# Layer 1's attention: who issues the small transfers of its softmax sums

## The chip, the cores and the metric
The program runs on one core of one Trainium2 chip. The metric is the device time of a run in microseconds (us); of several runs the median is given. One run was recorded by the hardware profiler, and its trace is read below.

The engines of the core each work through their own queue of instructions in order: TensorE (PE in the rows; its weight loads are PEld), VectorE (DVE), ScalarE (ACT), GpSimd (POOL) and SyncE (SP; SPq is its queue). They meet at semaphores alone.

## The reference
A decoder of four layers over x, 2 batches x 1024 positions x 256 channels. Each layer adds self-attention, cross-attention and a feed-forward part, with a layer norm behind each. The change lies in the self-attention of layer 1 alone: 16 query heads, 4 key/value heads, head size 64, rotary positions, causal.

```python
q, k, v = x @ Wq, x @ Wk, x @ Wv          # 16, 4 and 4 heads of 64, rotated q and k
att = softmax(mask(q @ k.T / 8))          # causal, per head
x = layernorm(x + (att @ v) @ Wo)
```

## The kernel before
`packed_attention` works in 32 **steps**. A step is 2 heads, one batch and 512 queries. Steps alternate: a step over the first 512 positions has 4 **units** (a unit is 128 keys against the step's queries), one over the last 512 has 8. They are called short and long steps here. In units that the causal mask cuts, fewer queries are left: 512, 384, 256, 128 over the last four units of every step, so for both heads together 1024, 768, 512 and 256 columns.

For each unit PE computes transposed scores (L914, mask L917); ACT takes the exponential twice, once to float16 (`ph_hi`, L1031) and once to float32 (`probs`, L1032; the trace calls this buffer `res`); the difference of the two is `ph_lo`. GpSimd subtracts it for three units of four (L834), VectorE for the fourth (L1093). PE then multiplies by the values (`values`, L935) and adds up the probabilities with a matrix of ones (`totals`, L955), two units behind and two units at a time.

Beside this, two steps ahead, PE computes the scores again in rows (L886, mask L889) only for VectorE to take their maxima (L1055). PE and VectorE take turns through two PSUM banks: item `a` of PE waits until VectorE is done with item `a - 2`. The maxima are turned (L894), split in two halves (L1063, L1065) and sent by SP into the query operand (L806). The order of these items among the units is laid out ahead by `Plan.lay`.

The end of a step goes through several engines:

- ACT waits for the step's `totals` and copies the output (`o_raw`, L1007) and the row sums (`sums`, L1011) out of PSUM. In its queue this stands ahead of the exponentials of unit 2 of the next step (`LAG = 2`).
- The sums lie along the free dimension of two partitions for each half. Two DMAs spread them over 128 partitions x 8 (`y_col`); they are GpSimd's (L839; L845 for the last step), in its queue behind unit 2's subtraction.
- VectorE adds the halves (L1076) and inverts (L1078) at the end of the next step's last unit.
- A DMA brings the inverse back into two rows (`r_row`, GpSimd's L842, behind the subtraction of unit 1 of the step after; L848 for the last two).
- PE spreads the rows over the partitions (L898, three steps behind), and VectorE multiplies the output by it (L1069).

SP's queue holds, for each step, the two transfers of the maxima, and at every second step nine loads of queries and keys for a coming pair of steps (L791, L794).

Of the kernel before, what the change touches and what calls it, by code (L numbers as in the profile page):

```python
# [683 lines left out]
def packed_attention(k, name, plan, G, stack, q, kk, v_all, o_t, kv_of=1, q_pos=None, k_pos=None, gate=None, split=False, scratch=None):  # L684
# [22 lines left out]
    S, U = len(steps), len(units)  # L707
    PR = G // 2
    GB = T // QC
    LEAD, INV, SPR = plan.lead, plan.invert_at, plan.spread_at  # L710
    pairs = not own_sums and G == 2
    SR = P // 4
    SLOTS = 5 if split else 4 if pairs else 3
    LAG = 2 if split else 0
    FULL = 3

    def by_dve(n):

        return n % 4 == 3
# [6 lines left out]
    KEEP = SPR + 1  # L726
# [15 lines left out]
    with Phase(k, name) as ph:  # L742
# [9 lines left out]
        sums = None if own_sums else scratch[:, in_scratch:in_scratch + 2 * QC].rearrange("p (i q) -> p i q", q=QC) if split else ph.sb("sums", [P, 2, QC])  # L752
        ones = None if own_sums else ph.sb("ones", [P, SR], F16 if split else F32)
        y_col, r_col = ph.sb("y_col", [P, 2, KEEP, YC]), ph.sb("r_col", [P, KEEP, YC])
        r_row = ph.sb("r_row", [P, KEEP, QC])
# [4 lines left out]
        y_ld = [ph.sem(f"y_ld{i}") for i in range(KEEP)]  # L760
        r_ld = [ph.sem(f"r_ld{i}") for i in range(KEEP)]
# [5 lines left out]
        s_ = ph.s  # L767
        EV = 1 if own_sums else 2
        n_clear = 1 if own_sums else 2

        with nc.Block() as block:

            @block.sync
            def _(sp):

                def load(tb):

                    st = steps[2 * tb]
                    slot = tb % LOADS
                    if tb >= LOADS:  # L780
                        sp.wait_ge(s_["b_done"], PR * plan.first_unit[2 * (tb - LOADS) + 2])
                    else:
                        sp.wait_ge(s_["k_filled"], slot + 1)
                        sp.wait_ge(s_["q_filled"], slot + 1)
                    h0, b = st.heads[0], st.batch
                    sp.sem_inc(s_["loading"], 1)
                    hk = h0 // kv_of
                    for c, r0, part in stack.q_parts:
                        rows = q[part][h0 * dh:(h0 + G) * dh].rearrange("(h d) n -> d h n", d=dh)
                        for g in range(GB):  # L790
                            sp.dma_start(qs[r0:r0 + dh, slot, c, g, :, :], rows[:, :, b * T + g * QC:b * T + (g + 1) * QC]).then_inc(ld[slot], 16)  # L791
                    for c, r0, part in stack.k_parts:
                        rows = kk[part][hk * dh:(hk + KH) * dh].rearrange("(h d) n -> d h n", d=dh)
                        sp.dma_start(ks[r0:r0 + dh, slot, :, c, :], rows[:, :, b * plan.n_keys:(b + 1) * plan.n_keys]).then_inc(ld[slot], 16)  # L794
                    if q_pos is not None:
                        for g in range(GB):
                            rows = q_pos[h0:h0 + G, :, b * T + g * QC:b * T + (g + 1) * QC]
                            sp.dma_start(qs[99:102, slot, 0, g, :, :], rows.rearrange("h r n -> r h n")).then_inc(ld[slot], 16)
                        sp.dma_start(ks[96:99, slot, :, 0, :], k_pos[h0:h0 + G, :, b * T:(b + 1) * T].rearrange("h r n -> r h n")).then_inc(ld[slot], 16)

                def maximum_rows(s):

                    st = steps[s]
                    sp.wait_ge(s_["maxed"], turned_at[s])
                    for i, m in enumerate((mh, ml)):
                        sp.dma_start(qs[R + i:R + i + 1, (s // 2) % LOADS, stack.m_chunk, st.q0 // QC, :, :], m[:, s % LEAD, :]).then_inc(m_ld[s % LEAD], 16)  # L806

                sp.dma_start(spread[:], k.a["c_spread"][0 if G == 4 else 1]).then_inc(s_["c_ld"], 16)
                for tb in range(min(LOADS, TBS)):
                    load(tb)  # L810
                for s in range(S):
                    maximum_rows(s)
                    tb = (s - LEAD - 1) // 2 + LOADS
                    if s >= LEAD and s % 2 and tb < TBS:
                        load(tb)

            @block.gpsimd
            def _(pool):
                for i in range(LOADS):
                    pool.memset(ks[stack.m0:R + 2, i, :, stack.m_chunk, :], 1.0).then_inc(s_["k_filled"], 1)  # L820
                pool.wait_ge(s_["k_filled"], LOADS)
                pool.memset(r_row[:], 0.0).then_inc(s_["cleared"], 1)
                if not own_sums:
                    pool.wait_ge(s_["cleared"], 1)
                    pool.memset(ones[:], 1.0).then_inc(s_["cleared"], 1)
                pool.wait_ge(s_["cleared"], n_clear)
                if split:
                    pool.wait_ge(s_["v_upper"], 1)
                    pool.tensor_tensor(v_lo[:], v_all[:], v_hi[:], ALU.subtract).then_inc(s_["v_lower"], 1)
                    for n, (s, u) in enumerate(units):  # L830
                        w = QC - u.off
                        if not by_dve(n):
                            pool.wait_ge(s_["exps"], n + 1)
                            pool.tensor_tensor(ph_lo[:, n % SLOTS, :, 0:w], probs[:, n % FULL, :, 0:w], ph_hi[:, n % SLOTS, :, 0:w], ALU.subtract).then_inc(s_["low_pool"], 1)  # L834
                        at = n - plan.first_unit[s]
                        if at == LAG and s:
                            pool.wait_ge(s_["evac"], EV * s)
                            for half in range(2):
                                pool.dma_start(y_col[:, half, (s - 1) % KEEP, :], sums[half * G * SR:(half + 1) * G * SR:SR, (s - 1) % 2, :]).then_inc(y_ld[(s - 1) % KEEP], 16)  # L839
                        if at == 1 and s >= 2:  # L840
                            pool.wait_ge(s_["recips"], s - 1)
                            pool.dma_start(r_row[0:G, (s - 2) % KEEP, :], r_col[:, (s - 2) % KEEP, :]).then_inc(r_ld[(s - 2) % KEEP], 16)  # L842
                    pool.wait_ge(s_["evac"], EV * S)
                    for half in range(2):
                        pool.dma_start(y_col[:, half, (S - 1) % KEEP, :], sums[half * G * SR:(half + 1) * G * SR:SR, (S - 1) % 2, :]).then_inc(y_ld[(S - 1) % KEEP], 16)  # L845
                    for s in (S - 2, S - 1):
                        pool.wait_ge(s_["recips"], s + 1)
                        pool.dma_start(r_row[0:G, s % KEEP, :], r_col[:, s % KEEP, :]).then_inc(r_ld[s % KEEP], 16)  # L848
                    return

                for n in range(S + INV - 1):
                    if n < S:
                        s, st = n, steps[n]
                        pool.wait_ge(s_["evac"], EV * (s + 1))
                        if own_sums:
                            pool.dma_start(y_col[:, 0, s % KEEP, :], o_raw[dh:P:MR, s % RAW, :]).then_inc(y_ld[s % KEEP], 16)
                        for half in range(0 if own_sums else parts_of(s)):
                            pool.dma_start(y_col[:, half, s % KEEP, :], sums[half * G * SR:(half + 1) * G * SR:SR, s % 2, :]).then_inc(y_ld[s % KEEP], 16)
                        if gate is not None:
                            b0 = st.batch * T + st.q0  # L860
                            raw = o_raw[:, s % RAW, :]
                            pool.tensor_tensor(raw, raw, gate[:, st.turn, b0:b0 + QC], ALU.mult).then_inc(s_["gated"], 1)
                    s = n - INV + 1
                    if s >= 0:
                        pool.wait_ge(s_["recips"], s + 1)
                        pool.dma_start(r_row[0:G, s % KEEP, :], r_col[:, s % KEEP, :]).then_inc(r_ld[s % KEEP], 16)
# [133 lines left out]
            def _(act):  # L1000

                def evacuate(s):

                    act.wait_ge(s_["values"], plan.first_unit[s + 1])
                    if s >= RAW:
                        act.wait_ge(s_["maxed"], spread_of[s - RAW])
                    act.activation(o_raw[:, s % RAW, :], X[s % 2], ACT.Copy).then_inc(s_["evac"], 1)  # L1007
                    if not own_sums:
                        if s >= 2:
                            act.wait_ge(y_ld[(s - 2) % KEEP], y_full[s - 2])  # L1010
                        act.activation(sums[:, s % 2, :], Y, ACT.Copy).then_inc(s_["evac"], 1)  # L1011

                if KR < P:
                    act.wait_ge(s_["zeroed"], 1)
# [2777 lines left out]
```

## Time and profile before

| | us |
|---|---|
| median of 3 runs | 3721.22 |
| lowest, highest | 3717.83, 3728.87 |
| profiled run, its own time | 3708.89 |
| its span in the trace | 3707.1 |
| layer 1's attention in the span | about 1283 to 1858 |

Over the whole span PE is busy for 2768.1 us (75%), VectorE 1767.4 (48%), ACT 1260.5 (34%), GpSimd 790.3 (21%). No ACT queue is among the DMA queues: all transfers of the kernel are issued by SP or GpSimd. Times in the rows are us from the span's start; "idle before" is how long an engine did nothing before that instruction, with the name of what it had waited for.

### The profile page before, as it was taken

To read this page: it belongs to the slowest core of one execution; us is meant where nothing else is said; L and a number is where in the kernel's file an instruction comes from. 1 tells how busy PE (TensorE), PEld (TensorE's weight loads), DVE (VectorE), ACT (ScalarE), POOL (GpSimd) and SP (SyncE) were. 2 spreads that over 40 slices of the span, in tenths; PEclk is the share of its full clock that TensorE was granted. 3 is DMA by queue.
4 is the path that set the end of the run, shared out by engine and by line. 5 is a ranking of instruction groups with operands and counts; after the bars stand their busy time and mean duration, and the time that the engine had idled before them with its cause. 6 is when DMAs were issued, how large, how long until landed. Compare 5 with 4: busy or idle time off the path is not lost. (4 is left out here: it accounts for less than half of the span.)

```text
span 3707.1 us, 42704 instructions
## 1 busy us (share of the span) xinstructions
PE 2768.1 (75%) x15498; PEld 1576.0 (43%) x15498; DVE 1767.4 (48%) x3896; ACT 1260.5 (34%) x2532; POOL 790.3 (21%) x648
## 2 busy tenths in 40 slices
PE   6789995786715688788774878787566888668696
PEld 3333333565512333333362455464342333346575
DVE  4566645244654555555424458144323767523412
ACT  4234441332411255565502300223212445335421
POOL 0101110134372456665600100002001000001100
PEclk9889997897867889999986979898787899789898
DMA  2211101600553322222102100200004020110132
GB/s 98 82 38 37 37 2 41 223 20 12 165 99 83 97 39 40 29 41 41 3 18 66 24 15 11 100 10 20 12 4 90 13 36 14 38 60 1 38 107 69
DMA packets 157229, 183.04 MB, mean 49 GB/s; under 512 B 34654, under 2 KB 123311, under 8 KB 156259
## 3 DMA queue, kind: packets, MB, share of 16 engines
q1 hardware_dynamic: 144547, 166.82, 15.6%
q0 software_dynamic: 12480, 13.57, 3.9%
q8 instruction: 122, 2.00, 0.2%
q14 instruction: 80, 0.66, 0.1%
HBM read 121.81 MB, written 61.59 MB: 49 GB/s over the span
## 5 line engine op out<-in xcount | busy, mean ns | idle before, releaser
L834 POOL TENSOR_TENSOR l1a_p_lo<-res,l1a_p_hi 128x1024 f16<-128x1024 f32 x144 | 266.9, 1855 | 211.5 <-ACT res L1032 211.3
L1055 DVE TENSOR_REDUCE l1a_nmax<-ps 128x1 f32<-128x512 f32 (+3 forms) x384 | 200.1, 551 | 149.0 <-PE ps L889 119.3
L1055 DVE TENSOR_REDUCE l0a_nmax<-ps 128x1 f32<-128x512 f32 (+3 forms) x384 | 200.9, 555 | 122.2 <-PE ps L889 93.3
L1055 DVE TENSOR_REDUCE l3a_nmax<-ps 128x1 f32<-128x512 f32 (+3 forms) x384 | 199.3, 553 | 80.5 <-PE ps L889 65.8
L1039 ACT ACTIVATE l0a_probs<-ps 128x1024 f32<-128x1024 f32 (+1 forms) x192 | 145.7, 812 | 229.7 <-PE ps L917 182.1
L1031 ACT ACTIVATE l1a_p_hi<-ps 128x1024 f16<-128x1024 f32 x192 | 158.1, 823 | 161.0 <-PE ps L917 135.3
L1039 ACT ACTIVATE l3a_probs<-ps 128x1024 f32<-128x1024 f32 (+1 forms) x192 | 148.8, 810 | 184.1 <-PE ps L917 147.9
L886 PE MATMUL ps<-l1a_ks,l1a_qs 128*128 128x512 f16 (+3 forms) x384 | 124.5, 345 | 95.7 <-DVE l1a_nmax L1055 74.7
L914 PE MATMUL ps<-l1a_qs,l1a_ks 128*128 128x512 f16 (+3 forms) x768 | 167.6, 333 | 21.9 <-ACT res L1032 21.9
L889 PE MATMUL ps<-mask,ident_b 128*128 128x128 bf16 x768 | 171.7, 231 | 0.0
L886 PE MATMUL ps<-l3a_ks,l3a_qs 126*128 126x512 f16 (+3 forms) x384 | 126.7, 354 | 44.9 <-DVE l3a_nmax L1055 20.0
L1032 ACT ACTIVATE res<-ps 128x1024 f32<-128x1024 f32 x192 | 158.7, 826 | 0.0
L917 PE MATMUL ps<-mask_t,ident_b 128*128 128x128 bf16 x768 | 154.5, 222 | 0.0
L886 PE MATMUL ps<-l0a_ks,l0a_qs 102*128 102x512 f16 (+3 forms) x384 | 124.9, 353 | 29.2 <-DMA l0a_ks<-l_k_pos 16.9
L2485 PE MATMUL ps<-x_m_all,res 128*128 128x512 f32 (+2 forms) x256 | 97.6, 528 | 21.2 <-PEq L111 14.2
L1667 PE MATMUL ps<-res,l1p_w 128*128 128x512 f32 x160 | 83.1, 681 | 34.9 <-DVE l1p_tmp L1730 22.9
L886 PEld LDWEIGHTS ps<-l1a_ks,l1a_qs 128*128 128x128 f16 x384 | 37.6, 98 | 168.2 <-DVE l1a_nmax L1055 111.5
L886 PEld LDWEIGHTS ps<-l0a_ks,l0a_qs 102*128 102x128 f16 x384 | 36.0, 99 | 169.7 <-DVE l0a_nmax L1055 122.9
L886 PEld LDWEIGHTS ps<-l3a_ks,l3a_qs 126*128 126x128 f16 x384 | 36.5, 99 | 156.4 <-DVE l3a_nmax L1055 113.0
L914 PEld LDWEIGHTS ps<-l1a_qs,l1a_ks 128*128 128x128 f16 x768 | 61.9, 99 | 92.9 <-issue 35.6
L914 PE MATMUL ps<-l3a_qs,l3a_ks 128*128 128x512 f16 (+3 forms) x384 | 99.4, 330 | 0.9 <-ACT l3a_probs L1039 0.9
L914 PE MATMUL ps<-l0a_qs,l0a_ks 104*128 104x512 f16 (+3 forms) x384 | 99.0, 331 | 0.5 <-ACT l0a_probs L1039 0.5
(671 smaller groups left out, 6279.2 us busy)
## 6 DMA issues: line engine op xcount, KB each, us to landing
f_w<-in_L_ffn_w_dram SPq DMA_DIRECT2D x16, 1024.0 KB, 7.4
f_slots<-x0a_zeros SPq DMA_DIRECT2D x32, 256.0 KB, 4.9
f_xe<-f_slots SPq DMA_DIRECT2D x32, 256.0 KB, 3.0
f_ys<-f_y SPq DMA_DIRECT2D x32, 256.0 KB, 2.3
l1a_qs<-l_q_h SPq DMA_DIRECT2D x64, 128.0 KB
d_wall<-in_L_ffn_W_dram SPq DMA_DIRECT2D x3, 2112.0 KB
l0a_qs<-l_q_h SPq DMA_DIRECT2D x32, 128.0 KB
l0a_ks<-l_k_h SPq DMA_DIRECT2D x16, 256.0 KB
```

What stands on the lines that cost most here:

```text
L834: pool.tensor_tensor(ph_lo[:, n % SLOTS, :, 0:w], probs[:, n % FULL, :, 0:w], ph_hi[:, n % SLOTS, :, 0:w], ALU.subtract).then_inc(s_["low_ ...
L886: ins = pe.matmul(sa[:, col:col + f.w], qs[0:stack.max_rows, slot, 0, st.q0 // QC, f.p, q0:q0 + P], ks[0:stack.max_rows, slot, f.p if KH > ...
L889: ins = pe.matmul(sa[:, f.w - P:f.w], k.ident_b[:], k.mask[:], start=False, stop=True)
L914: ins = pe.matmul(SB[x % 2][:, half, 0:w], ks[0:r, slot, p if KH > 1 else 0, d, u.key:u.key + KR], qs[0:r, slot, d, st.q0 // QC, p, u.off: ...
L917: ins = pe.matmul(SB[x % 2][:, half, 0:P], k.ident_b[:], k.mask_t[:], start=False, stop=True)
L1031: act.activation(ph_hi[:, n % SLOTS, :, 0:w], SB[n % 2][:, :, 0:w], ACT.Exp)
L1032: act.activation(probs[:, n % FULL, :, 0:w], SB[n % 2][:, :, 0:w], ACT.Exp).then_inc(s_["exps"], 1)
L1039: act.activation(probs[0:KR, n % SLOTS, 2 * pr:2 * pr + 2, 0:w], SB[x % 2][:, :, 0:w], ACT.Exp).then_inc(s_["exps"], 1)
L1055: dve.tensor_reduce(nmax[:, s % LEAD, f.chunk, f.p, f.tile:f.tile + f.n], src, AX.X, ALU.max, negate=True).then_inc(s_["maxed"], 1)
L1667: ins = pe.matmul(slot[j % 2][:, c0:c0 + w], lhsT, rhs, start=n == 0, stop=n == len(terms) - 1)
L2485: ins = pe.matmul(S[:, c:c + w], xs[:, d, t * P:(t + 1) * P], m_all[:, d, i, c:c + w], start=d == 0, stop=d == DC - 1)
```

## The change
In layer 1's attention (`split`), ACT issues the two DMAs of the sums itself, right behind its own copy of them and after waiting for that copy's semaphore; unit 2's exponentials come behind them. SP issues the DMA of the inverse, after the transfers of the maxima of its iteration `s` and ahead of that iteration's loads, for step `s - 3`; the last three follow at the end. GpSimd's queue keeps its subtractions alone. The other attentions keep their code.

```diff
@@ SP @@
+                def inverse_row(s):
+                    sp.wait_ge(s_["recips"], s + 1)
+                    sp.dma_start(r_row[0:G, s % KEEP, :], r_col[:, s % KEEP, :]).then_inc(r_ld[s % KEEP], 16)
                 for s in range(S):
                     maximum_rows(s)
+                    if split and s >= LEAD + INV:
+                        inverse_row(s - LEAD - INV)
                     tb = (s - LEAD - 1) // 2 + LOADS
                     if s >= LEAD and s % 2 and tb < TBS:
                         load(tb)
+                for s in range(S - LEAD - INV, S) if split else ():
+                    inverse_row(s)
@@ GpSimd @@
-                        at = n - plan.first_unit[s]
-                        if at == LAG and s:
-                            pool.wait_ge(s_["evac"], EV * s)
-                            for half in range(2):
-                                pool.dma_start(y_col[...], sums[...]).then_inc(y_ld[(s - 1) % KEEP], 16)
-                        if at == 1 and s >= 2:
-                            pool.wait_ge(s_["recips"], s - 1)
-                            pool.dma_start(r_row[...], r_col[...]).then_inc(r_ld[(s - 2) % KEEP], 16)
...
@@ ACT, evacuate(s) @@
                         act.activation(sums[:, s % 2, :], Y, ACT.Copy).then_inc(s_["evac"], 1)
+                        if split:
+                            act.wait_ge(s_["evac"], EV * (s + 1))
+                            for half in range(2):
+                                act.dma_start(y_col[:, half, s % KEEP, :], sums[half * G * SR:(half + 1) * G * SR:SR, s % 2, :]).then_inc(y_ld[s % KEEP], 16)
```

## Rows read from the trace of the kernel before

**Rows 1.** Busy time of each engine over 28 full steps, and TensorE's granted clock.
```profile
core 0: us, PE busy (x) PEld busy (x) DVE busy (x) ACT busy (x) POOL busy (x), PEclk, DMA share, GB/s
1340.00:1823.00 483.00, 390.37 (x3235) 180.99 (x3234) 263.45 (x531) 278.50 (x394) 299.49 (x211) 0.98 0.23 34
```

**Rows 2.** Waits of the stage: engine and line, releaser: us, times, longest.
```profile
POOL l1a_p_lo L834 <- ACT res L1032: 211.3, 122, 18.1
...
PE ps L886 <- DVE l1a_nmax L1055: 72.9, 59, 2.5
DVE l1a_y_col L1076 <- DMA l1a_y_col<-res: 51.3, 15, 4.2
...
PE ps L914 <- ACT res L1032: 21.9, 32, 1.8
```

**Rows 3.** Timeline, copies in a short step: start, us, engine, line.
```profile
1514.36 0.59 ACT L1011 ACTIVATE res<-ps 128x512 f32<-128x512 f32 x1
...
1514.74 0.60 SPq L794 DMA_DIRECT2D l1a_ks<-l_k_h  x1
...
1514.83 0.61 ACT L1031 ACTIVATE l1a_p_hi<-ps 128x512 f16<-128x512 f32 x1
...
1515.31 0.62 ACT L1032 ACTIVATE res<-ps 128x512 f32<-128x512 f32 x1
...
1516.07 1.02 PE L914 MATMUL ps<-l1a_qs,l1a_ks 128*128 128x512 f16 x4 [0.45 <-ACT res L1032]
```

**Rows 4.** Timeline, the end of the same short step.
```profile
1517.12 1.58 POOL L839 DMA_DIRECT2D l1a_y_col<-res  x2
...
1517.77 0.40 DVE L1093 TENSOR_TENSOR l1a_p_lo<-res,l1a_p_hi 128x256 f16<-128x256 f32 x1
...
1519.76 0.59 PE L886 MATMUL ps<-l1a_ks,l1a_qs 128*128 128x512 f16 x2
...
1521.27 0.17 DVE L1076 TENSOR_TENSOR l1a_y_col<-l1a_y_col 128x8 f32<-128x8 f32 x1 [3.10 <-DMA l1a_y_col<-res]
...
1521.59 1.83 DVE L1055 TENSOR_REDUCE l1a_nmax<-ps 128x1 f32<-128x512 f32 x3
...
1522.29 0.39 PE L886 MATMUL ps<-l1a_ks,l1a_qs 128*128 128x512 f16 x1 [1.93 <-DVE l1a_nmax L1055]
```

**Rows 5.** The same place in the first and the last of 14 short steps.
```profile
1348.78 0.59 PE L886 MATMUL ps<-l1a_ks,l1a_qs 128*128 128x512 f16 x2
...
1351.19 1.84 DVE L1055 TENSOR_REDUCE l1a_nmax<-ps 128x1 f32<-128x512 f32 x3
...
1797.48 0.59 PE L886 MATMUL ps<-l1a_ks,l1a_qs 128*128 128x512 f16 x2
...
1799.30 1.83 DVE L1055 TENSOR_REDUCE l1a_nmax<-ps 128x1 f32<-128x512 f32 x3
```

**Rows 6.** Timeline, copies in the long step that follows.
```profile
1525.52 0.59 ACT L1011 ACTIVATE res<-ps 128x512 f32<-128x512 f32 x1
...
1526.00 1.03 ACT L1031 ACTIVATE l1a_p_hi<-ps 128x1024 f16<-128x1024 f32 x1
...
1528.00 0.60 PE L914 MATMUL ps<-l1a_qs,l1a_ks 128*128 128x512 f16 x2 [0.77 <-ACT res L1032]
```

**Rows 7.** Issues by line or tile, ns min/median/max; then issue to landing, us: maxima's, sums'.
```profile
L806 SPq DMA_DIRECT2D l1a_qs<-l1a_mh x32: 623/634/731, 1301.1 to 1819.4; - x32
L806 SPq DMA_DIRECT2D l1a_qs<-l1a_ml x32: 620/656/1250, 1301.9 to 1820.0; - x32
...
L242 SPq DMA_DIRECT2D x3c_n_wb<-in_L_xattn_g_x_dram x1: 359/359/359, 3228.1 to 3228.1; - x1
...
DMA to landing us min/median/max: 1.6/1.8/3.9
...
DMA to landing us min/median/max: 2.7/3.3/3.9
```

**Rows 8.** Timeline, the end of the stage.
```profile
1846.01 0.59 ACT L1011 ACTIVATE res<-ps 128x512 f32<-128x512 f32 x1
...
1851.26 0.17 DVE L1076 TENSOR_TENSOR l1a_y_col<-l1a_y_col 128x8 f32<-128x8 f32 x1 [6.56 <-DMA l1a_y_col<-res]
...
1854.87 2.04 PE L898 MATMUL ps<-l1a_r_row,l1a_spread 128*128 128x512 f32 x2 [0.56 <-DMA l1a_r_row<-l1a_r_col]
```

More of the change, by code:

```diff
@@ L834, in _ @@
                             pool.tensor_tensor(ph_lo[:, n % SLOTS, :, 0:w], probs[:, n % FULL, :, 0:w], ph_hi[:, n % SLOTS, :, 0:w], ALU.subtract).then_inc(s_["low_pool"], 1)
-                        at = n - plan.first_unit[s]
-                        if at == LAG and s:
-                            pool.wait_ge(s_["evac"], EV * s)
-                            for half in range(2):
-                                pool.dma_start(y_col[:, half, (s - 1) % KEEP, :], sums[half * G * SR:(half + 1) * G * SR:SR, (s - 1) % 2, :]).then_inc(y_ld[(s - 1) % KEEP], 16)
-                        if at == 1 and s >= 2:
-                            pool.wait_ge(s_["recips"], s - 1)
[L842 to L848, printed above, removed]
                     return
```

## Prediction
> **What bounds the kernel now.** I read the busy time by stretch first, to see whether one engine is full in this stage. It isn't: over the 28 steps from 1340 to 1823 us, PE is busy for 390.37 of 483 us (81%), at a granted clock of 0.98 of full speed, which is its 2.4 GHz level, while GpSimd is at 62%, ACT at 58% and VectorE at 55% [rows 1]. So the stage is a chain that runs through PE and leaves it where another engine is late. The waits say where [rows 2]: PE waits 72.9 us for VectorE's maxima and 21.9 us, 32 times, for ACT's exponentials. VectorE waits 51.3 us, in 15 of the 16 short steps, for the transfer of the sums. GpSimd waits 211.3 us for ACT and is hardly ever what others wait for. That is the second thing to see: the engine that the change relieves has time to spare; only the lateness of what it issues can matter.
>
> Then the timeline, at both places where ACT copies the sums. In the short step the copy ends at 1514.95 (1514.36 + 0.59); the next exponential had started at 1514.83, so ACT had work waiting. Its float32 half ends at 1515.93, and PE, idle for 0.45 us, starts the next scores at 1516.07 [rows 3]. In the long step it is the same: copy at 1525.52, exponential at 1526.00 without a gap, and PE idle for 0.77 us until ACT is done [rows 6]. The 32 waits of PE on ACT are these places, at 0.45 and 0.77 us, two for each pair of steps. Behind each copy ACT is what holds PE up, and whatever is put between copy and exponential is paid by PE in full.
>
> **The change part by part.**
>
> *GpSimd's three issues gone.* They take 0.79 us each for the sums (1.58 for two, [rows 4]). Nobody waits for GpSimd's next subtraction, which itself waits for ACT [rows 2]: 0 us. Its cover is that idle time of 211.3 us; were GpSimd full, three issues in each of 32 steps would be worth some 75 us.
>
> *The sums come earlier.* GpSimd issues at 1517.12, behind a subtraction; VectorE gets to the addition at 1518.17 (1517.77 + 0.40), waits 3.10 us, and starts its next maximum at 1521.59 [rows 4]. Not all of the 3.10 us is PE's loss. PE issued two maximum items at 1519.76; a free VectorE takes the first about 0.41 us after that (the first item's 0.38 us and the hand-over; an estimate). It took it 1.83 us after, so 1.42 us late, and PE's third item followed, at 1522.29 after 1.93 us of idling. The same difference over the 14 short steps that have maxima goes from 1.38 to 2.00 us (first: 1351.19 - 1348.78 - 0.41 = 2.00; last: 1799.30 - 1797.48 - 0.41 = 1.41 [rows 5]); the 14 add up to 23.6, or 1.68 each. The fifteenth short step that waits has no maxima left, so there is nothing to win.
>
> Will the transfer be there? ACT issues about 1515.1 and 1515.7. By the sums' own slowest landing, 3.9 us [rows 7], the second is there at 1519.6; the maxima's small transfers from SP landed after 1.8 us, 3.9 at most [rows 7]. VectorE, itself shifted by what ACT costs (below), arrives near 1519.7. So the stall goes: **-23.6 us**.
>
> *ACT's wait and two issues.* The trace has no transfer issued by ACT. Its nearest rows are SP's transfers of the maxima in this stage, which are as small and go between rows and partitions too: 0.634 and 0.656 us, so 1.29 us for two [rows 7]. With them go the overlap that copy and exponential have now (0.12 us: 1514.95 - 1514.83) and a semaphore hand-over from ACT's copy to its own queue, which I take at the 0.14 us between ACT's end at 1515.93 and PE's start [rows 3]. Sum: 0.12 + 0.14 + 1.29 = 1.55 us a copy. Queued behind it are unit 2's exponentials, then PE's scores two units on, and through PE's ordered queue the turn of the maxima, the values and the totals. There is no slack after it: PE was idle for ACT already. 31 copies lie inside the stage (steps 1 to 31; the last is counted below): 31 x 1.55 = **+48.1 us**.
>
> Bounds of an issue: the shortest 128-partition one of small pieces, 0.359 us, and the longest of the maxima's, 1.25 us [rows 7]. That gives 0.98 and 2.76 us a copy, so +30 and +86 us. I take 1.55 because the maxima's medians hold 64 issues of this stage. A gain from this part is excluded; below the lower bound lies only an issue that doesn't stop ACT's queue, which is a rival.
>
> By the Trainium skill, "DMA: Bandwidth & Descriptors", section "Issuing engines are not separate DMA queues", the issuing sequencer's time is "usually small relative to the DMA itself"; taken as nothing, it would leave 0.26 us a copy and a gain of 18 us. Here the rows have 0.63 us of issue against 1.8 us to landing, a third, which is not small for ACT.
>
> *SP's transfer of the inverse.* One issue of about 0.63 us in each iteration. VectorE inverts at the end of the same step that ends the iteration's wait for maxima, so the added wait is short (before, the inversion comes 0.2 us behind the last addition). Queued behind it are nine loads. Their last starts at 1514.74 in rows 3 and would start at 1515.4, end at 1516.0; the next maxima's transfers aren't due before 1517.8, and the loads themselves serve a pair of steps further on. The inverse is used a whole step after it is issued. 0 us; without that cover it would be 0.66 us for each of 13 loads, 9 us.
>
> *The end of the stage.* Here all is on the path. ACT's copy ends at 1846.60 [rows 8]; its second issue would start near 1847.4. With a landing between 1.8 and 3.3 us, VectorE adds at 1849.2 to 1850.7 instead of 1851.26. SP then issues the inverse at once; GpSimd took 3.4 us from the addition's 0.17 us to PE's start at 1854.87 (with the reciprocal), and SP's 1.8 to 2.9 us of landing with 0.25 of arithmetic makes that 2.1 to 3.2. Together 0.8 to 3.6; I take **-2.3 us**.
>
> Sum: 48.1 - 23.6 - 2.3 = +22.2 us. Against the profiled run's own 3708.89 (1.8 above its span of 3707.1) that is 3731.1. The median of the runs stands 12.3 us above the profiled run, so the forecast is 3721.2 + 22.2 = **3743.4 us** (+0.6%).
>
> **The rivals.**
>
> *ACT's issue stops its queue only briefly: faster.* It decides at (23.6 + 2.3) / 31 = 0.84 us a copy, so at 0.29 us an issue with 0.26 beside it. If an issue costs some 0.1 us, a copy costs 0.46 and the sum is 14.3 - 25.9 = -12, 3710; if it costs nothing, -18, 3703. For it: no row shows ACT issuing. Against it: of the rows cited none is under 0.36, and SP's next issue always starts only when the one before has ended.
>
> *Cheap but not free: no change.* At 0.36 to 0.45 us an issue the sum is +4 to +10 us, 3726 to 3731. For it: simple transfers over 128 partitions take 0.36 us; against it: these cross partitions, as the maxima's do, at 0.63.
>
> *The two queues share what makes the descriptors: slower still.* In short steps SP would be issuing its last loads (until 1516.0) while ACT issues (from 1515.1). If one must let the other finish, each of ACT's two waits up to 0.6 us; with 0.9 us for both, 14 short steps add 12.6 us: 3756. Long steps have no loads at that point. In the rows, a few issues of the maxima reach 1.25 us, twice the median, with loads in flight. The Trainium skill, "Perfetto Trace Analysis", section "DMA Instruction — HWDGE (DVE, Sync)", has the generator shared by two sequencers and locked while in use; no run here shows ACT beside SP.
>
> *The sums land late all the same.* If ACT's transfers, in the middle of SP's loads, land only at 5.5 us or more, the stall stays and the 23.6 us are not won: +46, 3767. For it: the loads are in flight just then; against it: the longest landing of either kind is 3.9.
>
> **How the numbers follow.** Forecast 0.50 (with 0.5 to 0.8 us an issue: +14 to +33, 3735 to 3754). Shared generator 0.12, late landing 0.09. Cheap 0.14, brief or free 0.15. Faster by over 0.3% (11 us, about what a measurement tells from no change) comes from the last, 0.13; within 0.3% from the rest of it and from cheap, 0.16; slower 0.71. The range for 8 in 10 goes from 3709, which takes in part of the brief case, to 3770, which takes in both slower rivals and most of the upper bound of 1.25 us an issue (+60).
>
> **What the changed profile would show.** ACT's issue in its own rows, 0.6 us each, twice behind every copy. The exponential of unit 2 starts 1.4 us or more after the copy's end, and PE's wait on ACT rises from 21.9 us to about 65. VectorE's wait for the sums shrinks from 51.3 us to next to nothing. A pair of steps is longer by 2 x 1.55 - 1.68 = 1.4 us. The prediction is wrong if ACT's issues are under 0.3 us, if the exponential starts while they run, or if VectorE still waits for the sums.

## The result and the profile after

| | before | after |
|---|---|---|
| median, us (4 runs each) | 3723.64 | 3751.34 |
| lowest, highest | 3717.83, 3728.87 | 3750.23, 3754.62 |
| profiled run, span | 3708.89, 3707.1 | 3750.23, 3748.5 |

The ratio is 1.0078, with a 95% interval from 1.0062 to 1.0095: 0.8% slower, 27.7 us. The forecast was 3743.4 us, from 3709 to 3770, slower with a chance of 0.71.

The two profiled runs are 41.4 us apart, more than the medians, since the profiled run of the kernel before was faster than its four others. From the stage's first output copy to its last product they differ by 27.8 us. Another 12.0 us lie behind the stage, where the kernels are the same: the 11 profiled runs of this document need between 1849.4 and 1866.5 us for that part.

Three answers of the changed kernel's trace tell most of it. First the tile view of the sums' transfer, now in ACT's queue (ns min/median/max).

```profile
L1010 ACTq DMA_DIRECT2D l1a_y_col<-res x64: 503/520/1113, 1326.3 to 1879.8; - x64
```

An issue by ACT costs 0.52 us, less than the 0.645 that the forecast took from SP (the mean of 0.634 and 0.656 [rows 7]). Then the waits of the stage, in which VectorE waits for the sums only once, 4.5 us at its end:

```profile
POOL l1a_p_lo L843 <- ACT res L1031: 316.7, 137, 18.0
...
PE ps L909 <- ACT res L1031: 64.5, 32, 3.1
...
PE ps L881 <- DVE l1a_nmax L1054: 39.2, 60, 2.4
...
DVE l1a_y_col L1075 <- DMA l1a_y_col<-res: 4.5, 1, 4.5
```

Against [rows 2]: PE waits 42.6 us longer for ACT (64.5 us, forecast at about 65) and 33.7 us less for VectorE's maxima; GpSimd, relieved of 96 issues, waits 105 us longer for ACT and wins nothing. Last the timeline of a short step, the place of [rows 3]:

```profile
1531.40 0.59 ACT L1006 ACTIVATE res<-ps 128x512 f32<-128x512 f32 x1
...
1532.02 1.19 ACTq L1010 DMA_DIRECT2D l1a_y_col<-res  x2
...
1532.42 0.60 SPq L794 DMA_DIRECT2D l1a_ks<-l_k_h  x1
...
1533.33 0.60 ACT L1030 ACTIVATE l1a_p_hi<-ps 128x512 f16<-128x512 f32 x1 [1.34 <-issue]
...
1534.56 1.02 PE L909 MATMUL ps<-l1a_qs,l1a_ks 128*128 128x512 f16 x4 [1.90 <-ACT res L1031]
```

From copy to exponential it was 0.47 us and is 1.93. This is one of the dearer places: the pair of issues takes 1.19 us here, and in 27 of the 31 copies it takes 1.06 to 1.12 us and the exponential starts 1.80 to 1.87 us after the copy's start. So the usual price is 1.33 us a copy, against 1.55 forecast. PE idles 1.90 us at this place where it had idled 0.45. And behind such an idle stretch comes what the forecast had left out. These are four stretches from one output copy of ACT (`o_raw`) to the next: a short and a long one in which the clock falls, and one of each at full clock; the last figures of a row are the granted clock, the DMA share and GB/s, the first ones its length and PE's busy time.

```profile
1530.90:1543.73 12.83, 10.07 (x73) 4.01 (x72) 6.21 (x15) 6.60 (x10) 4.88 (x3) 0.87 0.22 62
1543.73:1567.52 23.79, 20.32 (x160) 9.28 (x158) 11.17 (x25) 13.39 (x18) 11.34 (x7) 0.93 0.07 19
1567.52:1578.79 11.27, 8.49 (x73) 3.70 (x72) 6.21 (x15) 6.60 (x10) 4.88 (x3) 1.00 0.26 71
1399.02:1422.71 23.69, 18.73 (x160) 8.95 (x158) 12.65 (x25) 13.39 (x18) 11.80 (x7) 1.00 0.08 19
```

The two short stretches hold the same work. In one the granted clock averages 0.87: TensorE was at its lower level, 1.2 GHz in place of 2.4, for some 3 us from about 1535.8 on, 1.2 us after the 1.90 us of idling had ended, and the stretch took 1.56 us longer. Seven of the 15 short stretches have such a fall, where before it was one; of the 16 long ones 11 have it, before it was five.

### The profile page after: what moved, and what is told of

It is laid out like the page before. It is cut to its first block and busy times, and to the rows that moved or that the text cites. A ratio compares the mean times of both kernels' runs of the same rounds, so it can differ in the third digit from the quotient of the medians.

```text
span 3748.5 us, 42704 instructions
## 1 busy us (share of the span) xinstructions
PE 2808.1 (75%) x15498; PEld 1590.9 (42%) x15498; DVE 1758.1 (47%) x3896; ACT 1263.6 (34%) x2532; POOL 710.3 (19%) x552
## 5 line engine op out<-in xcount | busy, mean ns | idle before, releaser
L909 PE MATMUL ps<-l1a_qs,l1a_ks 128*128 128x512 f16 (+3 forms) x768 | 173.8, 342 | 64.5 <-ACT res L1031 64.5
```

The source lines that it names most:

```text
L909: ins = pe.matmul(SB[x % 2][:, half, 0:w], ks[0:r, slot, p if KH > 1 else 0, d, u.key:u.key + KR], qs[0:r, slot, d, st.q0 // QC, p, u.off: ...
```

## The experiments

The ratios are to runs of the kernel before on the same chip. The column behind them is the time from the first to the last output copy of the stage in the profiled run, and then how many of the 16 long and 15 short stretches show a clock under 0.96. Both come from one execution of each kernel, and the falls differ between executions: two kernels below that leave PE's waits almost as they were have 3 and 2 falls where the kernel before has 6.

| kernel | ratio (95%) | copies, us | falls, long and short |
|---|---|---|---|
| before | | 522.0 | 5, 1 |
| changed | 1.0078 (1.0062 to 1.0095) | 553.0 | 11, 7 |
| ACT's part alone | 1.0085 (1.0063 to 1.0107) | 557.5 | 15, 9 |
| inverse by SP alone | 1.0004 (0.9990 to 1.0018) | 517.3 | 3, 0 |
| sums by SP, behind the loads | 0.9954 (0.9931 to 0.9977) | 514.7 | 9, 0 |
| four issues by ACT | 1.0237 (1.0208 to 1.0265) | 622.7 | 16, 15 |
| ACT's wait alone | 0.9997 (0.9982 to 1.0012) | 519.4 | 2, 0 |
| ACT issues later | 0.9948 (0.9928 to 0.9969) | 507.3 | 10, 0 |
| sums by SP, ahead of the loads | 0.9960 (0.9947 to 0.9973) | 507.5 | 11, 0 |
| the same, and VectorE's wide subtraction moved | 0.9832 (0.9819 to 0.9845) | 462.6 | 0, 0 |
| that subtraction moved alone | 0.9919 (0.9898 to 0.9940) | 498.6 | 0, 8 |

**Which half of the change.** The first kernel keeps ACT's part and leaves the inverse with GpSimd; the second keeps SP's part and leaves the sums with GpSimd.

```diff
 # ACT's part alone: the kernel before, and
+                        if split:
+                            act.wait_ge(s_["evac"], EV * (s + 1))
+                            for half in range(2):
+                                act.dma_start(y_col[...], sums[...]).then_inc(y_ld[s % KEEP], 16)
 # inverse by SP alone: the kernel before, and
+                    if split and s >= LEAD + INV:
+                        inverse_row(s - LEAD - INV)
```

> ACT issues the sums' two transfers, GpSimd keeps the inverse's. Theory (the loss is ACT's wait and two issues ahead of unit 2's exponentials, 1.46 us a copy by the changed kernel's rows, 31 times, less 23.6 us of VectorE's stall, more some us of lower clock): as the changed kernel, 3751 us, ratio to before 1.006 to 1.009. Rival (a part of the loss is SP's added wait and issue ahead of its loads): at least 8 us less than the changed kernel, ratio under 1.005.

> SP issues the inverse's transfer, GpSimd keeps the sums'. Theory: SP's queue has time, so only the stage's end gains, about 0.5 us: ratio 0.998 to 1.001. Rival (SP's wait holds up loads or maxima): ratio over 1.002, and waits of PE for query or key loads in the trace.

Both came out as the theory had it: 1.0085 and 1.0004. The whole loss is in ACT's part, and SP's added wait and issue cost nothing that can be measured (the interval ends at +0.2%).

**What in ACT's part.** One kernel adds to the kernel before nothing but ACT's wait for its own copy. The other cuts each transfer of the changed kernel in two, so that ACT issues four.

```diff
 # ACT's wait alone: the kernel before, and
+                        if split:
+                            act.wait_ge(s_["evac"], EV * (s + 1))
 # four issues
-                                act.dma_start(y_col[:, half, s % KEEP, :], sums[half * G * SR:(half + 1) * G * SR:SR, s % 2, :]).then_inc(y_ld[s % KEEP], 16)
+                                for g in range(G):
+                                    r0 = (half * G + g) * SR
+                                    act.dma_start(y_col[g * HALF:(g + 1) * HALF, half, s % KEEP, :], sums[r0:r0 + 1, s % 2, :]).then_inc(y_ld[s % KEEP], 16)
```

> The kernel before, with nothing but ACT's wait for its own copy added behind the copy; GpSimd still issues everything. Theory (the wait costs the overlap of copy and exponential and a hand-over, some 0.2 to 0.3 us a copy, and the rest of the 1.46 us is the two issues): 31 x 0.25 = 8 us more than before, ratio 1.001 to 1.003. Rival (the wait itself is the larger part of the loss): ratio over 1.005.

> The changed kernel with each half's transfer cut in two, a row each: ACT issues four transfers behind each copy. Theory (the price is the issues' time in ACT's queue, 0.53 us each): 31 x 2 x 0.53 = 33 us more than the changed kernel, 3784, ratio to before 1.014 to 1.019; a little less if a half-size transfer is issued faster. Rival (the loss is the wait for the copy, or the clock, and not the issues): within 8 us of the changed kernel, ratio under 1.010.

The wait costs less than expected. In its trace the timeline of a short step's copy is

```profile
1523.51 0.59 ACT L1011 ACTIVATE res<-ps 128x512 f32<-128x512 f32 x1
1524.13 0.60 ACT L1033 ACTIVATE l1a_p_hi<-ps 128x512 f16<-128x512 f32 x1
```

so 0.62 us from copy to exponential in place of 0.47, 0.15 us a copy for overlap and hand-over together; PE's wait on ACT grows by 4.8 us in all, which the median can't tell from nothing. Of the usual 1.33 us a copy the other 1.18 come with the issues: 1.06 for the pair and 0.12 around it.

The four issues cost twice what was expected: the median is 66 us above the changed kernel's (3817.3 against 3751.3), not 33. A cut transfer is no cheaper to issue (median 0.617 us), so 4 x 0.62 - 1.06 makes 1.4 us a copy, some 43 us for 31, of the 69.8 us by which the time between first and last copy grew. The rest, some 27 us, goes with the clock: now every stretch has a fall, 33.2 and 42.2 us of stretch times lacking clock against 20.1 and 13.4 in the changed kernel (each stretch's time by one less its clock, summed over the long and the short ones). The issues' time is the price, as the theory has it, but the clock adds to it.

**Where the issues stand.** The same two issues by ACT, moved behind the exponential of unit 3 in a short step and of unit 4 in a long one:

```diff
-                        if split:
-                            act.wait_ge(s_["evac"], EV * (s + 1))
-                            ... (the two issues)
+                        if s and n - plan.first_unit[s] == (3 if len(steps[s].units) == 4 else 4):
+                            send(s - 1)      # the wait and the two issues
```

> The changed kernel with ACT's wait and two issues moved behind later exponentials: behind unit 3's in a short step and unit 4's in a long one, where ACT was idle for 0.73 and 1.08 us in the rows of before. Theory (the price is not the issues but that they stand ahead of work that PE waits for): a long step pays about 0.15 us, a short one 0.5; VectorE's stall goes mostly, so ratio to before 0.993 to 0.998. Rival (ACT's queue pays wherever the issues stand): ratio 1.004 or more.

The ratio is 0.9948: the same work in the same queue is a gain. ACT still issues in 0.52 us (median 522 ns), but PE's wait on ACT is back at 22.4 us (21.9 before [rows 2]), and 13 of the 15 short stretches come to 9.80 or 9.81 us where they were 11.12 to 12.52. The timeline of one short step shows where the issues went:

```profile
1485.16 0.50 ACTq L1012 DMA_DIRECT2D l1a_y_col<-res  x1
1485.31 0.62 ACT L1033 ACTIVATE res<-ps 128x512 f32<-128x512 f32 x1
1485.69 0.54 ACTq L1012 DMA_DIRECT2D l1a_y_col<-res  x1
1485.79 0.42 ACT L1032 ACTIVATE l1a_p_hi<-ps 128x256 f16<-128x256 f32 x1
```

They don't lie in idle gaps of ACT, which was the expectation: they run beside its exponentials. The last row is an exponential that stands ahead of both issues in the program and starts after them, so ACT had been handed it before. In all 31 places the exponentials start where they did in the kernel before, to 0.02 us, and nothing is paid there, where 0.15 and 0.5 us a step were expected. The changed kernel has the same two issues, but ahead of them it waits for a copy that is just being made. When the copy ends, ACT has nothing else at hand, and the issues' whole length shows. So, as the rows of the three kernels read, neither the wait by itself (0.15 us) nor the issues by themselves (nothing) are the price; it is the issues behind a wait that lets ACT run empty.

**The stall of VectorE by itself.** SP issues the sums' transfers, once behind the nine loads of its iteration and once ahead of them:

```diff
 # behind the loads (the first of the two)
+                    if split and s >= LEAD:
+                        sum_columns(s - LEAD)      # wait for the copy, two issues by SP
 # ACT, in both
-                        if split: ... (the wait and the two issues)
```

> The changed kernel, but SP issues the sums' transfers too, behind the loads of its iteration; ACT issues nothing. Theory: the stall of VectorE goes or shrinks below 1 us and ACT pays nothing, so the 23.6 us are won alone, with 2 to 3 at the stage's end: about 3698, ratio 0.992 to 0.995. Rival (the stall was hidden by what PE waits for next, and the 23.6 us are not there to win): ratio 0.999 to 1.001.

> As the kernel in which SP issues the sums' transfers, but ahead of the loads of its iteration, not behind them. Theory (there VectorE still stalled in 13 steps, because the sums stood behind nine loads; and where they landed after GpSimd's next subtraction had begun, the addition itself took 1.5 to 2 us): no stall, every short stretch at 9.8 us, 15 x 1.6 = 24 us less than before and 3 at the end, ratio 0.991 to 0.995, and 4 to 8 us below the other. Rival (the loads, now up to 6 us later, hold up the maxima two steps on): PE waits for loads, and the ratio is over 0.996.

Both are faster than before, so the stall was real. But the first won 0.5%, less than the 0.5 to 0.8% expected (its ratio lies just outside). Its profiled run was also the slowest of its eight (3721.2 us, median 3706.0), so its trace shows the bad side. Its sums were issued about 1 us late, behind the loads, and in eight short stretches VectorE stalled anew. The timeline of one such step, and below it one in which the sums came in time:

```profile
1422.58 2.12 POOL L853 TENSOR_TENSOR l1a_p_lo<-res,l1a_p_hi 128x1024 f16<-128x1024 f32 x1 [2.07 <-ACT res L1037]
...
1423.27 1.46 DVE L1081 TENSOR_TENSOR l1a_y_col<-l1a_y_col 128x8 f32<-128x8 f32 x1 [1.75 <-DMA l1a_y_col<-res]
...
1523.97 0.17 DVE L1081 TENSOR_TENSOR l1a_y_col<-l1a_y_col 128x8 f32<-128x8 f32 x1 [0.59 <-DMA l1a_y_col<-res]
...
1524.45 2.13 POOL L853 TENSOR_TENSOR l1a_p_lo<-res,l1a_p_hi 128x1024 f16<-128x1024 f32 x1 [2.07 <-ACT res L1037]
```

The addition of eight columns takes 0.17 us alone and 1.46 us when it starts inside a subtraction of GpSimd; it ends at 1424.73, when that ends (1424.70). By the Trainium skill, "SBUF — State Buffer", section "Who interferes with whom", a VectorE instruction with two inputs in SBUF contends with a GpSimd instruction that reads SBUF; this trace agrees. So a sum that lands 1.2 us later costs 2.5 us of VectorE's time, and the stretch 1.3 us (11.1 for 9.80). With the sums ahead of the loads all 14 short stretches are at 9.80 or 9.81 us and no wait for a query or key load shows up: the price of loads issued up to 6 us later is nothing.

And still that kernel's ratio is 0.9960, where 0.991 to 0.995 was expected, and its stage is 14.5 us shorter and not 24. The long stretches give the difference back: 11 of them are at 23.9 or 24.0 us with a clock of 0.93, where before it was five; at full clock they take 22.38. 6 more times about 1.55 us makes 9.

**What the fall of the clock follows.** In those long stretches PE idles 2.35 us for VectorE, which does its one 1024-column subtraction in 2.70 us. It starts inside one of GpSimd's (1430.62 to 1432.75 at this place); alone, as in the last long step, the same subtraction takes 1.22 us.

```profile
1431.12 2.70 DVE L1098 TENSOR_TENSOR l1a_p_lo<-res,l1a_p_hi 128x1024 f16<-128x1024 f32 x1
```

Moving this one subtraction in each long step to GpSimd leaves VectorE the 256-column ones:

```diff
     def by_dve(n):
-        return n % 4 == 3
+        return n % 4 == 3 and units[n][1].off > 0
```

> As the kernel in which SP issues the sums ahead of its loads, and GpSimd also takes the 1024-column subtraction of every long step that VectorE had (VectorE keeps the 256-column ones). There VectorE's subtraction took 2.70 us because it waited for GpSimd's, PE idled 2.35 us for it, and behind that the granted clock was at half speed for 3 to 4 us in 11 of 16 long stretches. Theory (this wait, and the clock that follows it, ate a good part of what the short steps won): PE's wait there falls under 1.3 us, the clock stays at 1.00, a long stretch falls from 22.4 or 23.9 to about 21.5, ratio to before 0.984 to 0.990. Rival (GpSimd becomes the bound with a fourth subtraction of four): PE waits for GpSimd instead, ratio 0.995 or more.

> The kernel before with only that subtraction moved to GpSimd; the transfers are issued as before. Theory: 16 x 1.0 to 1.5 us for the wait and 5 x 1.5 us for the clock: ratio 0.993 to 0.996, less than the two together because GpSimd now issues the sums behind a later subtraction. Rival (nothing hangs on VectorE's wait for GpSimd): ratio 0.999 or more.

The first of these is 1.7% faster than the kernel before (median 3666.48 us), slightly more than the 1.0 to 1.6% expected. These are the waits of PE in its stage, and below them the length of 28 steps and each engine's busy time in them (PE first), with the granted clock, the DMA share and GB/s last:

```profile
PE ps L891 <- DVE l1a_nmax L1060: 23.3, 63, 0.6
PE ps L919 <- ACT res L1037: 22.4, 32, 1.8
```

```profile
1349.97:1771.60 421.63, 379.48 (x3210) 176.28 (x3209) 226.22 (x513) 277.02 (x392) 254.13 (x141) 1.00 0.14 39
```

No wait of PE for VectorE is longer than 0.6 us (2.5 before [rows 2]); no stretch between the copies has a fall; the long ones, but for the first and the last two, are at 20.40 or 20.41 us. PE is busy for 90% of the 28 steps (81% before). With the subtraction moved alone, in the kernel before, the ratio is 0.9919, also slightly beyond what was expected (0.993 to 0.996): a long stretch takes 20.5 us for 22.4, a gain of 1.9 where 1.0 to 1.5 was expected, and none has a real fall (the lowest shows 0.98). But eight of the short ones do, where before it was one, though VectorE's stall in them is the same. These two kernels take away the wait and the falls together, so they don't tell the price of a fall by itself.

## Why the prediction was right, and by how much by chance

The mechanism was right: two issues stood ahead of exponentials that PE waits for. The prediction charged them wherever "queued behind it" was work that PE needs; the kernel with the later issues shows that this holds only where ACT has run empty, as it has here. The terms, by the steps of the prediction; the measured ones are from one profiled run of each kernel:

| term | forecast, us | measured, us |
|---|---|---|
| ACT's wait and two issues | 31 x 1.55 = +48.1 | 16 x 1.28 + 15 x 1.32 = +40.3 |
| VectorE's stall gone | -23.6 | 14 x 1.6 = -22.4 |
| end of the stage | -2.3 | -3.2 |
| GpSimd relieved, inverse by SP | 0 | 0 |
| the clock | not in the sum | +13 |

- *ACT's price.* The step "1.55 us a copy" was 0.2 to 0.3 too high. The issue is 0.53 us (1.06 for two) and not 0.645; the wait cost 0.15 with the overlap, forecast at 0.26; and 0.12 us around the issues was forecast at nothing. That makes 1.33 us. At full clock a long stretch went from 22.41 to 23.69 us, 1.28 more. A short one without the stall is 9.80 (the kernels in which ACT doesn't pay) and with ACT's issues 11.12, 1.32 more.
- *The stall.* 11.4 us, the mean of 13 short stretches before at full clock, less 9.80 is 1.6; the forecast had 1.68 from the lateness of the first maximum. It also had VectorE finding the sums there, and it did in every step but the last.
- *The stage's end.* From the last output copy to the end of the last product it was 12.12 us (1845.52 to 1857.64) and is 8.88 (1878.15 to 1887.03).
- *The clock.* The sum had no term for it. From first to last copy the stage grew by 31.0 us, while 40.3 - 22.4 makes 17.9; the other 13.1 go with the falls. That they are the clock's is a remainder, not a measurement. Before, five long stretches and a short one lose 8.7 us by them. After, seven short ones lose 12.8 (six at about 12.8 for 11.12, and the first, 13.92), and the long ones 9. Most of these 9 lie in three of them: the first (2.9 us; its first issue also took 1.11 us), the second, in which the fall comes behind VectorE's wait as before (1.6), and the last (2.7). The last takes 3.98 us more than it did: PE idles 3.10 us on ACT there, and the clock is at half speed for some 7 us.
- In the other long stretches a fall costs far less than before: 23.79 us with it and 23.69 without, in the rows above (23.76 to 24.16 in seven of them, 22.92 for 22.42 in an eighth), where before it was 23.9 to 24.0 against 22.4. It now comes earlier, behind ACT's 2.09 us, and PE reaches VectorE's subtraction later. VectorE then does it in 1.22 us, outside GpSimd's, and PE waits 0.87 us for it, not 2.35. One loss hides in the other. So the 13 us can't be read as so many falls at one price.

So a term that was 8 us too high stood against one of 13 us that was missing, and the sum came out 5.5 us low: that it came so near is luck. The stage's 31.0 less 3.2 make 27.8 us, and the medians differ by 27.7, which is luck too. In the kernel with the inverse by SP alone, whose waits between the copies are those of before, the time from first to last copy is 4.7 us shorter than in the profiled run before, with three falls instead of six, while the medians agree.

Of the rivals, the brief or free issue is out (0.52 us, and ACT's exponential waits for it). The late landing is out. The shared generator does little: in 13 short steps SP issues loads while ACT issues its pair, and the pair takes 1.19 to 1.22 us in three of them (one is at 1532.02 above) and 1.06 to 1.12 in ten, as in the steps without loads. That is at most 0.16 us and not 0.9. SP's own issues beside it took their usual 0.60 us or little more, five of them 0.72 to 0.85.

What stays open: why one stretch has a fall and the next, with the same waits, has none. The rows show only what goes before, and the length of the last idle stretch doesn't decide it. The kernel with four issues, which idles 3 us and more at each copy, has a fall in every stretch, and the one whose PE idles over 1.4 us only twice (1.82 and 1.78 us) has none. But the changed kernel has a fall behind 1.77 us of idling (at 1819.10) and none behind 3.14 (at 1854.73); from 1.8 to 2.5 us both occur. Nor is it settled why the kernels without the short steps' stall have 9 to 11 falls in the long stretches and the kernel before five, at the same 2.35 to 2.39 us of idling, nor why the kernel with the subtraction moved alone has eight in the short ones and the kernel before one.

## What to carry to other kernels

A transfer's issue is work of the queue that it stands in. Before it is given to a compute engine, look for what waits for that engine's next instruction, and for whether the transfer waits for something that this engine has only just started. With the same two issues by ACT the kernel was 0.8% slower than before where they waited for the copy ahead of two exponentials, and 0.5% faster where the copy was long done and ACT had exponentials at hand. A queue that only issues, SP's, took them without a price even in front of nine loads, since those had time. And when a wait of TensorE grows to about 2 us, count more than the wait: in these kernels part of what came behind it ran at half speed, in some executions of the step and not in others.

## What the runs showed of the hardware that was not expected

- ACT issues a small transfer in 0.52 us (median of 64). Right behind its own copy the next exponential waits for the pair, 1.33 us in all; with exponentials already handed over, they run on beside the issues, undisturbed in 31 of 31 places. Cut in two, each half takes 0.62 us (median of 128): the issue doesn't get cheaper with size. The halves landed 1.6 to 3.2 us after the issue, 1.8 in the median.
- The same sums issued by GpSimd landed 2.7 to 3.9 us after the issue [rows 7]. Issued by SP at 1421.2 (the second of the two that start at 1420.62) they were there at 1423.27, 2.1 us after.
- A VectorE addition of 128x8 with both inputs in SBUF took 1.46 us when it started inside a GpSimd subtraction, 0.17 outside. The 1024-column one took 2.70 inside and 1.22 outside.
- TensorE's granted clock fell to its lower level around or behind idle stretches of 1.77 to 3.10 us, and stayed there for 3 to 7 us although PE was busy again; behind others just as long it didn't. 1.33 us more in ACT's queue became up to 3 us of a stretch in that way.
